# Score products of an attention kernel: operands of half height in pairs, or of full height one by one

## The reference, cut to what matters

```python
x_ = layer_norm(ctx_1024, ln1_g, ln1_b); l = layer_norm(_layernorm(x), ln2_g, ln2_b)
q = l @ Wq                                        # (16, 256, 1024)
k, v = jnp.split(jnp.concatenate([x_, l], axis=1) @ Wkv, 2, axis=-1)
q, k, v = (to_heads(q), to_heads(k), to_heads(v)) # 16 heads of 64
w = jax.nn.softmax(jnp.einsum('bhqd,bhkd->bhqk', q * scale, k * scale), axis=-1)
out = jnp.einsum('bhqk,bhkd->bhqd', w, v)         # then @ Wo
x = x + jnp.tanh(g_xattn[0]) * out
x = x + jnp.tanh(g_ffn[0]) * ffn(_layernorm(x))
```

## Time and profile before

| | |
|---|---|
| median of 3 runs | 1365.5 us (1364.32 to 1367.94) |
| profiled execution, its own time | 1364.59 us |
| its span | 1362.8 us |
| attention steps (first to last score product) | 36.7 to 1068.4 us |
| PE busy, share of the span | 1257.7 us, 92% |
| DVE busy | 900.1 us, 66% |
| ACT busy | 636.2 us, 47% |
| POOL busy | 738.3 us, 54% |
| granted TensorE clock, mean | 0.981 |

### The profile page before, as it was taken

The page is one execution under the profiler, slowest core; times in us unless marked ns, Lnnn a source line. Parts: engine busy times, 40 slices in busy tenths (PEclk is TensorE's granted clock), DMA queues, the critical chain, the costliest instruction groups (busy, mean ns, idle before and its releaser), DMA issues. The chain is left out here.

```text
span 1362.8 us, 28186 instructions
## 1 busy us (share of the span) xinstructions
PE 1257.7 (92%) x8982; PEld 1023.9 (75%) x8982; DVE 900.1 (66%) x2710; ACT 636.2 (47%) x1958; POOL 738.3 (54%) x894
## 2 busy tenths in 40 slices
PE   1899999999999999999999999999999886999996
PEld 1688888878787877778778878788888774877764
DVE  4566677776776777676767676777666564455464
ACT  2555555454554454555454545554555421333332
POOL 1655645666555666566565646565656412454444
PEclk9999999999999999999999999999999987999998
DMA  4950000000000000000000000000000601345656
GB/s 129 296 161 4 3 1 4 17 4 17 7 13 13 9 11 10 12 9 15 7 19 2 19 3 20 1 19 1 17 2 17 182 8 49 112 126 163 201 175 201
DMA packets 61823, 70.90 MB, mean 52 GB/s; under 512 B 7056, under 2 KB 56160, under 8 KB 61664
## 3 DMA queue, kind: packets, MB, share of 16 engines
q1 hardware_dynamic: 54464, 49.96, 12.7%
q0 software_dynamic: 6912, 18.95, 3.8%
q10 hardware_dynamic: 288, 0.00, 0.0%
HBM read 35.19 MB, written 33.70 MB: 51 GB/s over the span
## 5 line engine op out<-in xcount | busy, mean ns | idle before, releaser
L1087 POOL TENSOR_SCALAR probs<-probs,inv_sum 128x333 f32<-128x333 f32 x384 | 425.4, 1123 | 0.0
L1137 ACT ACTIVATE probs<-st,neg_max 128x333 f32<-128x333 f32 x512 | 268.8, 538 | 270.8 <-DVE neg_max L1276 270.8
L1084 POOL TENSOR_TENSOR probs<-probs,inv_sum 128x333 f32<-128x333 f32 x128 | 94.7, 740 | 403.4 <-DVE inv_sum L1287 403.1
L1276 DVE TENSOR_REDUCE neg_max<-st 128x2 f32<-128x666 f32 x256 | 205.9, 846 | 133.1 <-PE st L1369 133.1
L1353 PE MATMUL st<-ident,probs 128*128 128x128 f32 (+1 forms) x1536 | 204.1, 273 | 1.1 <-POOL probs L1087 1.1
L1388 PE MATMUL ov<-PT,V 128*64 128x256 f32 (+1 forms) x1536 | 197.5, 392 | 0.0
L1353 PEld LDWEIGHTS st<-ident,probs 128*128 128x128 f32 (+1 forms) x1536 | 182.8, 143 | 17.9 <-POOL probs L1087 1.4
L1323 PE MATMUL pj<-wkv,lT 128*128 128x512 f32 (+1 forms) x576 | 158.5, 411 | 16.1 <-DVE Q_hl L1296 15.9
L1369 PE MATMUL st<-K_hl,Q_hl 64*128 64x334 f32 x1536 | 153.1, 331 | 18.3 <-issue 8.9
L1308 DVE COPY PT<-st 128x512 f32<-128x512 f32 x256 | 163.8, 682 | 0.8 <-PE st L1353 0.8
L1388 PEld LDWEIGHTS ov<-PT,V 128*64 128x64 f32 (+1 forms) x1536 | 100.2, 138 | 64.7 <-issue 28.5
(11 more groups left out here) (175 smaller groups left out, 1729.6 us busy)
## 6 DMA issues: line engine op xcount, KB each, us to landing
slots_x<-zeros SPq DMA_DIRECT2D x10, 1032.0 KB, 13.5
V<-slots_x SPq DMA_DIRECT2D x80, 129.0 KB
yg<-routed_y SPq DMA_DIRECT2D x32, 256.0 KB, 3.2
out<-X SPq DMA_DIRECT2D x32, 128.0 KB
stage<-in_L_xattn_Wkv SPq DMA_DIRECT2D x4, 512.0 KB, 4.0
X<-in_x SPq DMA_DIRECT2D x2, 1024.0 KB, 13.9
w_gu<-in_L_ffn_expert_gate_w SPq DMA_DIRECT2D x2, 960.0 KB, 9.3
w_gu<-in_L_ffn_expert_up_w SPq DMA_DIRECT2D x2, 960.0 KB, 10.3
```

The costliest lines, as they stand in the source:

```text
L1084: pool.tensor_tensor(probs[:, v, 0, 0:SKV], probs[:, v, 0, 0:SKV], inv_sum[:, v, 0:1].to_broadcast([P, SKV]), ALU.mult).then_inc(normed, 1)
L1087: pool.tensor_scalar(probs[:, v, i, 0:SKV], probs[:, v, i, 0:SKV], inv_sum[:, v, i:i + 1], None, ALU.mult).then_inc(normed, 1)
L1137: nc.scalar.activation(probs[:, v, i, 0:SKV], st_bank(i)[:, 0:SKV], ACT.Exp, bias=neg_max[:, v, i:i + 1], accum_out=sums[:, v, i:i + 1]).t ...
L1276: nc.vector.tensor_reduce(neg_max[:, v, 2 * i:2 * i + 2], st[i][:, :, 0:SKV], AX.X, ALU.max, negate=True).then_inc(maxed, 1)
```

## The change

`Q_hl` gives way to two tensors of full height for each head: `Q_hh` holds the head's high part in both halves of the partitions, `Q_l0` its low part in the lower half over zeros. `K_hl` holds for each head the high part in the lower half and the low part in the upper. One product of `Q_hh` with `K_hl` sums high x high and high x low over 128 rows, one of `Q_l0` with it adds low x high. So a tile of queries and a head need two products instead of three, each of 128 rows.

```diff
@@ -620,7 +620,9 @@
 
 
     K_hl = sb("K_hl", [P, 2, 2, SKVE], F32R)
-    Q_hl = sb("Q_hl", [P, 2, 2, SQ], F32R)
+    Q_hh = sb("Q_hh", [P, 2, 2, SQ], F32R)
+    Q_l0 = sb("Q_l0", [P, 2, 2, SQ], F32R)
+    LOW, HIGH = slice(0, HALF), slice(HALF, P)
     V = sb("V", [P, NKT, INNER])
     neg_max = sb("neg_max", [P, 2, 4])
     sums = sb("sums", [P, 2, 4])
@@ -1146,7 +1148,10 @@
             if has(0):
                 n, bank, _, _ = filled("Q", PAIRS, bb, u)
                 act.wait_ge(pj_full, n + 1)
-                copy(Q_hl[:, r, 0, :], bank[:, 0:SQ], ACT.Copy, scale=SCALE).then_inc(q_hi, 1)
+                for head, own in enumerate((LOW, HIGH)):
+                    for to in (own, LOW if head else HIGH):
+                        last = copy(Q_hh[to, r, head, :], bank[own, 0:SQ], ACT.Copy, scale=SCALE)
+                last.then_inc(q_hi, 1)
             if isinstance(bb, int) and bb == 0 and u == 2:
                 for i in range(2):
                     act.wait_ge(wo_in[i], 16)
@@ -1154,7 +1159,9 @@
             if has(0):
                 n, bank, _, _ = filled("K", PAIRS, bb, u)
                 act.wait_ge(pj_full, n + 1)
-                copy(K_hl[:, r, 0, :], bank[:, 0:SKVE], ACT.Copy).then_inc(k_hi, 1)
+                for head, own in enumerate((LOW, HIGH)):
+                    last = copy(K_hl[LOW, r, head, :], bank[own, 0:SKVE], ACT.Copy)
+                last.then_inc(k_hi, 1)
             if p in V_STEPS and has(0):
                 kt, half = V_STEPS[p] % NKT, V_STEPS[p] // NKT
                 kn = KT[kt][1]
@@ -1179,6 +1186,7 @@
         for bank in pj_free:
             dve.sem_inc(bank, 1)
         dve.wait_ge(tables, 1)
+        nc.vector.memset(Q_l0[HIGH].rearrange("p a h q -> p (a h q)").bitcast(F32), 0.0)
 
         def layer_norm(j, part):
 
@@ -1293,13 +1301,16 @@
             if has(0):
                 _, bank, free, _ = filled("Q", PAIRS, bb, u)
                 dve.wait_ge(q_hi, PAIRS * bb + u + 1)
-                nc.vector.scalar_tensor_tensor(Q_hl[:, r, 1, :], bank[:, 0:SQ], SCALE,
-                                               Q_hl[:, r, 0, :].bitcast(F32), ALU.mult, ALU.subtract
-                                               ).then_inc(free, 1)
+                for head, own in enumerate((LOW, HIGH)):
+                    last = nc.vector.scalar_tensor_tensor(Q_l0[LOW, r, head, :], bank[own, 0:SQ], SCALE,
+                                                          Q_hh[own, r, head, :].bitcast(F32), ALU.mult, ALU.subtract)
+                last.then_inc(free, 1)
                 _, bank, free, _ = filled("K", PAIRS, bb, u)
                 dve.wait_ge(k_hi, PAIRS * bb + u + 1)
-                tt(K_hl[:, r, 1, :], bank[:, 0:SKVE], K_hl[:, r, 0, :].bitcast(F32), ALU.subtract
-                   ).then_inc(free, 1)
+                for head, own in enumerate((LOW, HIGH)):
+                    last = tt(K_hl[HIGH, r, head, :], bank[own, 0:SKVE], K_hl[LOW, r, head, :].bitcast(F32),
+                              ALU.subtract)
+                last.then_inc(free, 1)
             next_rows = p in L_STEPS and exists(b + 1) and exists(b)
             if has(LAG_T):
                 m, v = PAIRS * bb + u - LAG_T, (u - LAG_T) % 2
@@ -1363,11 +1374,10 @@
                     pe.wait_ge(pt_lo, 2 * (m - 1))
                     pe.wait_ge(pt_hi, m - 1)
                 for qt in range(QT):
-                    for n, (a, a_) in enumerate(((0, 0), (0, 1), (1, 0))):
-                        for head in range(2):
-                            own = slice(head * HALF, (head + 1) * HALF)
-                            last = mm(st_bank(2 * qt + head)[:, 0:SKVE], Q_hl[own, r, a, qt * P:(qt + 1) * P],
-                                      K_hl[own, r, a_, :], start=(n == 0), stop=(n == 2))
+                    for head in range(2):
+                        for n, q_part in enumerate((Q_hh, Q_l0)):
+                            last = mm(st_bank(2 * qt + head)[:, 0:SKVE], q_part[:, r, head, qt * P:(qt + 1) * P],
+                                      K_hl[:, r, head, :], start=(n == 0), stop=(n == 1))
                     last.then_inc(st_full, 1)
             if has(LAG_AV):
                 m, v, q = PAIRS * bb + u - LAG_AV, (u - LAG_AV) % 2, (u - LAG_AV) % PAIRS
```

## The result

| | before | after |
|---|---|---|
| median | 1366.4 us | 1570.1 us (1566.2 to 1578.5) |
| ratio | | 1.150 (95% interval 1.145 to 1.154) |
| span of the profiled execution | 1362.8 | 1566.7 |
| first to last score group | 36.7 to 1067.5 | 37.0 to 1271.3 |
| DVE busy | 900.1 | 1052.3 |

What follows compares the result with a forecast made beforehand. PE's work and a chain through ACT and DVE were taken as nearly equally long; lengthening the chain adds 7.10 us a batch, less 0.6 for entries, times 16: +104 on 1364.6, so 1469, range 1435 to 1502.

Steps and rivals of the forecast that it cites:

- the bound: PE's own work and a chain through ACT and DVE are nearly equally long; the change shortens neither and lengthens the chain.
- steps without V: Steps with no V product wait for DVE's `PT` copies; the one from 867.98 was to grow from 6.75 to 8.11 us.
- the pitch of the copies and splits: Starts of half-height copies on ACT 0.27 (Q) and 0.33 (K) apart, of DVE's splits 0.33 and 0.42, as before.
- V's start: In four of eight steps the V product starts at +6.08 us after the score group's start, before +5.17.
- the case where copies don't overlap: Rival, 8%: copies between different partitions hold ACT for their full 0.40 or 0.45 us; 60 us more, about 1530.
- the forecast's base: The forecast time of 1469 us, in which copies and splits keep the pitch of the rows.
- PE's longer score group adds nothing: Score group on PE takes 1.3 us instead of 1.11; its later end (+0.2) is covered by V's wait.
- a gain of 0.6 a batch on entry: Ahead of the score group, 0.1 us saved in each of the six steps that PE enters without waiting.
- the first two banks are full: First two score banks full at +0.45 us with the fourth product, against +0.41 with the third pair: 0.04 later.
- the rest of the sum: Step terms for the added copies, splits and products: 7.10 us a batch, less 0.6 for entries, 6.5; times 16, +104.
- Rows count, not columns: Rival, 6%: on ACT and DVE two half-height instructions together cost what one whole does; 1365 to 1370 us.
- The count of products pays: Rival, 2%: each score product has the array to itself, so four fewer save 77 us at most; 1288 us.

Runs made afterwards that it cites:

- copies_alone: Changed kernel with its half-height copies and splits kept, but twelve half-height score products in pairs as before; 1556.3 us (1.139).
- dup_late: Changed kernel with the two duplicating `Q_hh` copies on ACT moved behind K's two and read from `Q_hh` itself; 1459.3 us (1.068).
- half_in_place: Changed kernel with as many half-height copies and splits, all reading and writing only the lower half of the partitions; 1478.4 us (1.082).

## Why the prediction was wrong

**Right:** the bound. Pairs of half-height products share the array; the change saves PE nothing; V waits for Q's split in nearly all steps, steps without V for the `PT` copies; the experts' stage is unmoved. `copies_alone` and `dup_late` show that the chain, not busy time, carries the loss.

**Wrong: the pitch of the copies and splits.** The step was "I take the rows' own pitch, since in all of them columns set the price" (0.27, 0.33, and 0.33 and 0.42 on DVE). Measured: 0.39, 0.46, 0.43, 0.52. V's start then moves from +6.08 to +6.59: 0.36 from three copies' starts, 0.10 from DVE, the rest from the banks being full later. In steps without V, 8.93 instead of 8.11. In runs, everything that hangs on changed starts, the clock's 22 us with it, is 1570 - 1478 = 92 us. The nearest rows could not show this, since nearly every instruction in them starts at partition 0. I let them stand for operations that don't, and gave the case where copies don't overlap only 8%, priced it on ACT alone, and left it out of the range. That rival gave 1530. DVE's part adds 0.1 before each V product and 0.3 before the scores of the steps without V: (6 x 0.1 + 2 x 0.3) x 16 = 19; with the clock's 22 it comes to 1571. That this meets the measured 1570 to 1 us is luck in part: the sum starts from the forecast's base, and `half_in_place` measured that base 9 us higher. From 1478 the same terms give 1579.

**Wrong: nothing was said of the clock.** PE stood idle ahead of the scores for 1.5 to 2.6 us behind the steps without V, and during or within 1.5 us behind two thirds of these waits the granted clock fell to 0.50; 22 us.

**Wrong in size: the score group.** "PE's longer score group adds nothing" and a gain of 0.6 a batch on entry: measured +16 us by itself, 1.0 a batch, and 14 on top of the copies. Of the gain the part ahead of the group was there (0.09); the 0.11 inside it was missing in most steps (the second product follows after 0.23). So the group takes 1.40 and not 1.3, and the first two banks are full 0.13 later (+0.54 against the third pair at +0.41) and not 0.04. Each step's chain starts from there: 0.09 x 128 = 12 us.

**Right by the run that isolates it:** the rest of the sum. With unchanged starts the four copies, two copies and four splits and the products give 1478 against 1469 forecast, and the banks' 12 us cover the difference. The agreement hides one more error: the sum takes 6.75 us for the step without V in every batch, and in four it is 8.5 to 8.9 in the kernel before (the one that ends at 413.21). In after those steps take 8.9 to 9.2, so there the change adds 0.2 to 0.5 and not 1.36.

*Rows count, not columns* fell: half-height copies 0.26 apart, like whole ones of 256 columns. *The count of products pays* fell: 1382.8 with the products alone, slower.

## What to carry to other kernels

Before splitting one instruction into parts of the partitions, ask three things: does it stand in the chain that ends a wait, do the parts start where their neighbours start, and is there a copy that can be made later. Two products of half height that run side by side on the array take the time of one of full height (0.15 us here), so eight full ones against twelve halves is more work and not less: it cost 16 us even with operands that came for nothing. The count of products, twelve against eight, says the opposite. An engine at half load can hold the longest chain: moving two copies past two others, with no work saved, was worth 111 us with the clock's share, and moving one copy and one split in the kernel before gave 11 (0.8%).

## What the runs showed of the hardware that I had not expected

- ACT holds an instruction until the one before has ended if its input or its output starts at another half of the partitions: 0.39 us instead of 0.27 for 256 columns, 0.46 instead of 0.33 for 334; either change alone is enough. Half height at the same start overlaps as full height does (0.26). Only starts at 0 and 64 were tried.
- DVE does the same: 0.43 instead of 0.33 to 0.34, 0.52 instead of 0.41 to 0.42.
- After 2.2 us in which TensorE had nothing to do, twelve products took 2.76 us instead of 1.45, at a granted clock of 0.50; ten products without use in such gaps kept the clock (1.00 instead of 0.96 and 0.97) and made the kernel 22 us faster.
- The first score product of full height keeps 0.22 us or more to the second in five of a batch's eight steps, though the tiling doesn't change before it, and 0.15 to 0.17 in the three whose score group starts 0.12 after the last `yb` product. What it waits for was not tried.
- Ahead of the group half-height products cost 0.09 us more: 0.21 from the last `yb` product to the first of them, 0.12 to the first of full height.
